# A perceiver block on one core: x and the context also loaded by columns, and the start, the end of the attention and the feed-forward part rearranged

## What is computed

```
x = x + xattn(layernorm(x), ctx)       # ctx has 128 keys, causal mask: query q sees keys <= q, so keys 64..127 never count
x = x + attn(layernorm(x))             # keys and values rebuilt through a 32-wide latent; scores clipped, times a decay, softmax
x = x + ffn(layernorm(x))              # 128 -> 512 -> GELU -> 128
# in ffn both linears quantise input and weight per tensor: q = round(x / scale), scale = max|x| / 127, over the whole tensor
```

## Time and profile before

| | us |
|---|---|
| median of 3 runs | 324.59 |
| lowest, highest | 322.42, 324.89 |
| the profiled execution's own time | 324.61 |
| its span (first to last instruction) | 322.8 |

### The profile page before, as it was taken

The page is one execution under the profiler, slowest core; times in us unless marked ns, Lnnn a source line. Parts: engine busy times, 40 slices in busy tenths (PEclk is TensorE's granted clock), DMA queues, the critical chain, the costliest instruction groups (busy, mean ns, idle before and its releaser), DMA issues.

```text
span 322.8 us, 13785 instructions
## 1 busy us (share of the span) xinstructions
PE 292.3 (91%) x5792; PEld 205.0 (64%) x5792; DVE 256.5 (79%) x561; ACT 250.1 (77%) x544; POOL 226.9 (70%) x176
## 2 busy tenths in 40 slices
PE   4796989999999999999999999999999998575884
PEld 3455757676767676867677777776667767321363
DVE  1486587899977887888788887878788998679883
ACT  3485795868687988787889898889877877499583
POOL 5177576874969697879999999999989970055000
PEclk9798999999999999999999999999999999759999
DMA  8999000000000000000000000000000000000027
GB/s 194 229 199 198 3 2 2 2 4 3 4 2 4 2 4 4 2 4 2 2 4 4 4 4 2 4 3 4 4 2 4 4 3 5 2 0 0 0 66 196
DMA packets 19102, 9.54 MB, mean 30 GB/s; under 512 B 5153, under 2 KB 18786, under 8 KB 19042
## 3 DMA queue, kind: packets, MB, share of 16 engines
q1 hardware_dynamic: 18322, 8.25, 12.0%
q10 hardware_dynamic: 720, 0.43, 0.6%
HBM read 6.57 MB, written 2.10 MB: 27 GB/s over the span
## 4 chain that ended last, share of the span: by engine, by line
PE 75%; ACT 14%; DVE 4%; issue 3%; DMA 1%; ACTq 1%; SPq 0%; DVEq 0%
PE ps L554 13%; PE ps L535 11%; PE ps L581 9%; PE ps L587 8%; PE ps L597 8%; PE ps L475 5%; ACT arena L860 4%; PE ps L459 4%; PE ps L468 4%; PE ps L552 4%; PE ps L566 3%; PE ps L645 2%; PE ps L441 2%; ACT arena L775 2%; DMA arena<-in_ctx 1%
## 5 line engine op out<-in xcount | busy, mean ns | idle before, releaser
L782 ACT ACTIVATE pt<-ps 128x512 f32<-128x512 f32 x128 | 75.9, 594 | 21.7 <-PE ps L554 20.7
L386 POOL TENSOR_TENSOR u<-u,mx 128x1024 f32<-128x1024 f32 x32 | 60.8, 1902 | 37.1 <-DVE mx L991 36.9
L378 POOL TENSOR_TENSOR ud<-u,con 128x1024 f32<-128x1024 f32 x31 | 73.5, 2372 | 1.9 <-DVE u L977 1.9
L972 DVE SCALAR_TENSOR_TENSOR u<-ps,rs,arena 128x1024 f32<-128x1024 f32 x32 | 41.0, 1282 | 20.3 <-PE ps L535 20.2
L535 PE MATMUL ps<-arena,qT 32*64 32x256 f32 x1024 | 44.2, 401 | 6.4 <-ACT arena L775 4.3
L977 DVE TENSOR_SCALAR u<-ps 128x1024 f32<-128x1024 f32 x32 | 39.0, 1220 | 12.5 <-PE ps L535 12.1
L581 PE MATMUL ps<-pt,vx 128*32 128x64 f32 x2048 | 41.0, 221 | 1.7 <-DVE oT L918 1.5
L581 PEld LDWEIGHTS ps<-pt,vx 128*32 128x32 f32 x2048 | 32.2, 110 | 14.8 <-issue 10.0
L587 PE MATMUL ps<-pt,con 128*32 128x128 f32 x1024 | 40.0, 275 | 0.0
L991 DVE TENSOR_REDUCE mx<-u 128x16 f32<-128x1024 f32 x32 | 38.7, 1210 | 0.1
L535 PEld LDWEIGHTS ps<-arena,qT 32*64 32x64 f32 x1024 | 14.9, 129 | 32.2 <-issue 22.5
(11 more groups left out here) (153 smaller groups left out, 568.2 us busy)
## 6 DMA issues: line engine op xcount, KB each, us to landing
out<-pt SPq DMA_DIRECT2D x8, 256.0 KB, 2.3
x<-in_x SPq DMA_DIRECT2D x4, 256.0 KB, 3.6
arena<-in_ctx SPq DMA_DIRECT2D x8, 128.0 KB, 4.1
x<-in_x SPq DMA_DIRECT2D x2, 512.0 KB, 7.0
arena<-in_ctx SPq DMA_DIRECT2D x4, 256.0 KB, 6.6
arena<-in_mask_BxS_if SPq DMA_DIRECT2D x2, 256.0 KB, 5.7
arena<-in_mask_BxS_if SPq DMA_DIRECT2D x4, 64.0 KB, 3.9
arena<-in_mask_BxS_if SPq DMA_DIRECT2D x2, 128.0 KB, 3.8
```

What stands on the lines that cost most here:

```text
L378: pool.tensor_tensor(dh, uh, decay.unsqueeze(1).to_broadcast([P, H, HALF]), ALU.mult)\
L386: pool.tensor_tensor(uh, uh, mx[:, n % 4, 0:count].unsqueeze(2).to_broadcast([P, count, HALF]), ALU.subtract)\
L782: act.activation(pt[:, n % 2, 4 * half:4 * half + 4].rearrange("p h n -> p (h n)"), ps[:, bank, :], ACT.Exp).then_inc(s["emptied"], 1)
L972: dve.scalar_tensor_tensor(by_head(u[:, n % UB]), sc, rs[:, 0, n:n + 1], mask[:, n].unsqueeze(1).to_broadcast([P, H, HALF]), ALU.mult, ALU ...
```

## The change

- `kernel()` also passes x laid out by columns, 128 x 4096, and the first 64 keys of the context by columns, 128 x 4096. `ctx_1024` itself is no longer an input. SP's `load(n)` now issues context columns (into the arena), x columns (into xn3T, which layer one does not use otherwise), x. Pieces "x" and "c" of layer one are gone with their copies; q, k and v of layer one read the loaded columns.
- ACT issues wk, the constants without the identity, wq, the identity, wv. PE starts with 8 matmuls on a zeroed tile (WARM), and the first pieces are k, cq, q. `expand(0, 0)` on ACT comes after cq.
- The last tile's numerators use a bank of the scores (`num_den`); its division comes after the moments of tile 62. The last root is split (28 to 30, and 31).
- The last layernorm: group 6 and tiles 28 to 30 on POOL, tile 31 on DVE. The first maximum's transposes use bank OB and no longer wait for the last copy (L764).
- Up projection: no "minus 1536" pass; instead 32 `open_up` matmuls of 512 columns (weights times -1536) start each accumulation, 8 of them before the first step. The first and last GELU are in two halves. The GELU table is loaded at turn 69.
- Down projection: POOL sums the four blocks of w2 at turns 30 and 31, so one matmul replaces the four of `offset`, and the bias matmul moves to the opening (`open_down`); groups 4 to 7 are opened between later steps. Hidden rounding: ACT 1, 3, 5, 7; POOL 2, 6; DVE 0, 4.

```diff
-LEAD = (("v", 3), ("x", 8), ("c", 7), ("k", 6), ("q", 5))
+LEAD = (("v", 3), ("x", 8), ("k", 6), ("q", 5))
-         ((0, 8), (8, 8), (16, 8), (24, 4), (28, 4)))
-ROOT_TURN = (..., (46, 54, 62, 66, 69))
-APPLY3 = (50, 52, 58, 60, 63, 65, 66, 70)
+         ((0, 8), (8, 8), (16, 8), (24, 4), (28, 3), (31, 1)))
+ROOT_TURN = (..., (46, 54, 62, 66, 67, 69))
+APPLY3 = (50, 52, 58, 60, 63, 65, 67, 70)
-X_ACT = (1, 2, 3)
-H_ACT = (1, 2, 4, 5, 7)
-DVE_TAIL = (("a", 0), ("a", 3), ("f", 0), ("f", 1), ("a", 6)) + tuple(("f", g) for g in range(2, 8))
+WARM = 8
+X_ACT, X_DVE, X_POOL = (1,), (0, 2, 3), (4, 5, 6, 7)
+H_ACT, H_POOL = (1, 3, 5, 7), (2, 6)
+DVE_TAIL = (("a", 0), ("a", 4)) + tuple(("f", g) for g in range(8))
+GELUS = ((0, 0, 1), (0, 1, 2)) + tuple((k, 0, 2) for k in range(1, 15)) + ((15, 0, 1), (15, 1, 2))
...
-    pieces[-1] = [("x", 0), ("cq", 0), ("c", 0), ("q", 0), ("k", 0)]
-    early = ([("v", 0), ("x", 1), ("c", 1)], [("k", 1), ("q", 1)], [("v", 1), ("x", 2)], [("c", 2)], [("k", 2)],
-             [("q", 2)])
+    pieces[-1] = [("k", 0), ("cq", 0), ("q", 0)]
+    early = ([("v", 0)], [("k", 1), ("q", 1)], [("v", 1)], [], [("k", 2)], [("q", 2)])
...
+                sp.dma_start(cT[:, P * t0:P * t1], ctx_cols[0, :, P * t0:P * t1]).then_inc(C_IN[n], 16)
+                sp.dma_start(xn3T[:, P * t0:P * t1], x_cols[:, P * t0:P * t1]).then_inc(XT_IN[n], 16)
                 sp.dma_start(x[:, t0:t1], x_t[:, t0:t1]).then_inc(X_IN[n], 16)
-                for b in range(2):
-                    sp.dma_start(cx[HALF * b:HALF * (b + 1), t0:t1], ctx_t[b, 0:HALF, t0:t1]).then_inc(C_IN[n], 16)
...
+            def last_norm(g, tiles):
+                pool.wait_ge(RS[2], batch_of(2, tiles[-1]))
+                pool.wait_ge(s["filled"], gets_empty(("x3", g - 2)))
+                pool.wait_ge(s["amax_done"], g - 1)
+                for t in tiles:
+                    last = pool.tensor_scalar(xn3[:, g % 2, t % GT], x[:, t], mv[:, 2, t, 0:1], rs[:, 2, t:t + 1],
+                                              ALU.subtract, ALU.mult)
...
+            pool.wait_ge(s["ascale"], 2)
+            pool.wait_ge(s["xr_done"], len(X_DVE))
+            for g in X_POOL:
+                pool.tensor_scalar(x16[g], xn3T[:, g * GT * P:(g + 1) * GT * P], scal[:, 11:12], ROUND16, ALU.mult, ALU.add)
+            pool.wait_ge(s["hscale"], 2)
+            for g in H_POOL:
+                if g >= 6:
+                    pool.wait_ge(s["down_done"], g - 5)
+                pool.tensor_scalar(h16[g % 6], hidden[:, :, g * GT * P:(g + 1) * GT * P], scal[:, 19:20], ROUND16,
+                                   ALU.mult, ALU.add).then_inc(s["hr_done_pool"], 1)
...
+            def open_up(k):
+                for m in range(2):
+                    pe.matmul(ps[:, 2 * (k % 4) + m, :], w1qT[:, k % FC],
+                              minus_off[:, :].unsqueeze(1).to_broadcast([P, GT, P]), start=True, stop=False)
+            def open_down(g):
+                pe.matmul(ps[:, g, :], minus_off[:, :], w2s[:, :].unsqueeze(1).to_broadcast([P, GT, D]), start=True, stop=False)
+                pe.matmul(ps[:, g, :], ones_b[:, :], b2q[:, :].unsqueeze(1).to_broadcast([96, GT, D]), start=False, stop=False)
+            pe.wait_ge(s["warm_set"], 1)
+            for n in range(WARM):
+                pe.matmul(ps[:, OB, :], warm[:, 0:P], warm[:, :], start=True, stop=True)
...
+                if n == NS + LAG_ADD[1]:
+                    open_up(0)
+                    open_up(1)
...
-            pe.wait_ge(s["emptied"], max(fill.values()) + 1)
             pe.wait_ge(s["ared_local"], 1)
-            pe.transpose(ps[0:1, 0, 0:P], scal[:, 8:9], ident).then_inc(s["ared_row"], 1)
+            pe.transpose(ps[0:1, OB, 0:P], scal[:, 8:9], ident).then_inc(s["ared_row"], 1)
...
+            pe.wait_ge(s["emptied"], max(fill.values()) + 1)
+            open_up(2)
+            pe.wait_ge(s["ascale"], 1)
+            open_up(3)
```

More of the change, by code:

```diff
@@ L441, in piece @@
                         last = pe.transpose(ps[:, bank, i * P:(i + 1) * P], src[:, i], ident)
-                if kind == "c":
-                    pe.wait_ge(C_IN[CHUNK[g]], 32)
-                    bank = bank_of(what)
-                    for i in range(GT):
-                        last = pe.transpose(ps[:, bank, i * P:(i + 1) * P], cx[:, g * GT + i], ident)
                 if kind == "cq":
@@ L467, in piece @@
                     bank = bank_of(what)
-                    last = pe.matmul(ps[:, bank, :], wk[:, layer], (xT if layer else cT)[:, j % 2],
+                    last = pe.matmul(ps[:, bank, :], wk[:, layer], xT[:, j % 2] if layer else cT[:, j * GT * P:(j + 1) * GT * P],
                                      start=True, stop=True)
@@ L635, in _ @@
                 if k >= 4:
-                    pe.wait_ge(s["gelu_done"], k - 3)
+                    pe.wait_ge(s["gelu_done"], gelu_count(k - 4))
+                    open_up(k)
                 for m in range(2):
-                    n0 = (2 * pair + m) * GT * P
-                    last = pe.matmul(ps[:, 2 * (k % 4) + m, :], w1qT[:, c], xq[:, n0:n0 + GT * P],
-                                     start=True, stop=True)
-                last.then_inc(s["up_done"], 1)
-            def offset(g):
-                for c in range(FC):
-                    pe.matmul(ps[:, g, :], minus_off[:, :], w2qT[:, c].unsqueeze(1).to_broadcast([P, GT, D]),
-                              start=(c == 0), stop=False)
+                    g = 2 * pair + m
@@ new lines, in _ @@
+                    if c == 0 and g in X_DVE:
+                        pe.wait_ge(s["xr_done"], X_DVE.index(g) + 1)
+                    elif c == 0 and g in X_ACT:
+                        pe.wait_ge(s["xr_done_act"], X_ACT.index(g) + 1)
+                    elif c == 0:
+                        pe.wait_ge(s["xr_done_pool"], X_POOL.index(g) + 1)
+                    pe.matmul(ps[:, 2 * (k % 4) + m, :], w1qT[:, c], x16[g], start=False, stop=True)\
+                        .then_inc(s["up_done"], 1)
@@ L662, in _ @@
                 else:
-                    pe.wait_ge(s["hr_done_dve"], (1 if g == 0 else 1 + sum(e not in H_ACT for e in range(g + 1))))
+                    pe.wait_ge(s["hr_done_dve"], 1 if g == 0 else 3)
                 for i in range(GT):
@@ L833, in _ @@
                 weights(n)
+                if n == ROOT_TURN[2][-1]:
+                    act.activation(scal[:, 31:32], cst[:, 0:1], ACT.Gelu, bias=cst[:, 0:1])
                 if n == 24:
@@ L849, in _ @@
                             expand(j, h)
-            act.activation(scal[:, 31:32], cst[:, 0:1], ACT.Gelu, bias=cst[:, 0:1])
             act.wait_ge(s["ascale"], 2)
@@ L993, in _ @@
                 for tile in due(n, LAG_PV):
-                    if tile != EARLY:
+                    if tile not in (EARLY, NS - 1):
                         divide(tile)
```

246 lines of the change are left out of this document (142 added, 104 removed).

## The result

| | before | after |
|---|---|---|
| median (lowest to highest) | 324.74 us (322.42 to 325.02), 4 runs | 316.16 us (314.52 to 318.24), 4 runs |
| profiled execution: own time, span | 324.61, 322.8 | 315.6, 313.7 |
| forecast | | 309.5, range 305 to 315 |

What follows compares the result with a forecast made beforehand. PE's work in the attention was taken as the bound, with chains of little overlap at the start and before the first GELU. 324.6 - 3.9 (layer one) - 7.0 (start) - 4.2 (tail) = 309.5 us; range 305 to 315.

Steps and rivals of the forecast that it cites:

- Part 2: The start: loaded columns replace transposes and copies, so first reading and turn 4 come earlier; 7.0 us gained, bounds 3.4 and 9.
- Rival B: At the start, the extra bytes delay each chunk up to load 3; 313.1 us in all, chance 0.11.
- 0.7 for the clock: Around turn 4: PE still waits some 2.5 us before it, so half of the low clock's 1.5 us is gained.
- Part 1: Steady layer one, groups 4 to 7 without x and c pieces: 0.97 us saved a group, 3.9 in all.
- It fits, barely: Layer one, turns 10 to 16: DVE's 2.0 us of idle time suffices against about 1.5 that PE saves.
- Rival C: DVE becomes the bound of layer one, whose gain is then 1.9 us; 311.5 us in all, chance 0.08.
- Part 3: From the last values to the first GELU: POOL's norms become the limit, GELU starts 2.0 us earlier, bounds 0 and 3.
- Part 4: First GELU to the second maximum's transpose: 0.3 us from the halved GELU, 0.9 from fewer matmuls ahead of the transpose.
- Part 5: The down projection: engines would gain 2 us, the stores leave 1.0; bounds -2 and 2.
- 8 x 0.9: Down projection: PE does each of eight groups in 0.9 us, within 8.3 us from the first rounded half.
- ready well before PE is at groups 2 and 6: Down projection: POOL's two roundings, 2.8 us each, are done before PE needs them.
- rival A: Down projection: POOL and DVE shut each other out, DVE's second half waits for POOL's 2.8 us; 312.3 us, chance 0.21.

Runs made afterwards that it cites:

- experiment 4: The changed kernel with eight matmuls of zeros at the end of turn 3, where PE waits for ACT: 314.81 us, ratio 0.9729.
- experiment 1: The changed kernel with POOL's two roundings waiting for DVE's three: 312.47 us, ratio 0.964; with the groups also shared anew: 314.38 us, ratio 0.9713.
- inverse first: The changed kernel with ACT taking the inverse of the denominator ahead of the first exponent in layer one: 314.62 us, ratio 0.9728.
- the best one: The changed kernel with turn 3's fill, inverse first, last norms on DVE, POOL's rounding behind DVE's, new sharing, PE kept busy, eight output slots: 309.18 us.

## Why the prediction was right and where it was wrong

**Direction and cause** were right: the start and the groups of layer one carry the gain, and the time around the span is the same (1.8 and 1.9).

**Part 2** came out in its sum: 6.6 of 7.0. Read of the scores, the mask as its last wait and turn 4 were each met within 0.3 us; the first scores came at 9.19, not near 8.5, hidden behind the mask. Rival B fell: the queue moved 306 GB/s. But the sum holds an error that another one covers. The way to turn 4 gave 5.8 (5.5 forecast), and turns 4 to 7 gave 0.83 (20.48 to 19.65), where 1.0 for group 3's transposes and 0.7 for the clock had been counted. So of the 0.7 for the clock nothing came: the stretch at 0.50 was about as long as before (3.4 us, 3.2 before), and experiment 4 shows that 1.6 lay there. Half of the matmuls' low-clock time was the wrong model, as before turn 4 it all went or all stayed in each profiled run.

**Part 1** failed in its sentence "It fits, barely". The sum of DVE's idle time over seven turns was compared with the sum of PE's savings. But the savings come in single turns, behind a fixed order of DVE work of 1.28 + 0.28 + 1.21 + 0.28 us; idle time elsewhere in the window can't be used there. Rival C had the engine, and nearly the size (2.5 measured, 1.9 priced), at a chance of 0.08; its "only turns 10 to 16" was too narrow, as turns 9 and 21 lost time too. Also the pieces were priced too high: PE's busy time fell by 0.83 a group on average, not 0.97.

**Part 3** was right about POOL (the norms are its 5.5 us, and they hold the maximum), and its number is an error of adding: its own terms, 0.65 for the transpose and 0.9 to 1.4 less 0.3 behind it, give 1.25 to 1.75, not the 2.0 taken. Measured are 1.5, of which 0.84 come up to the transpose and 0.65 behind it, where the openings between the scale and the first data matmul took 1.89 us in part at low clock. **Part 4**: the 0.9 behind DVE's last maximum came (0.26 us are left of 1.19). The 0.3 in front didn't: DVE starts 0.4 sooner behind the first GELU's start, but its eighteen maxima end 18.8 us after their start instead of 18.1.

**Part 5** is the main failure, 3.1 us, by two steps. The step "8 x 0.9" took the full clock for granted. Taking away the `offset` matmuls ahead of the second maximum (counted as a gain in part 4) left PE idle for 3.1 us, and the down projection began at half the clock: 1.2. The second is "ready well before PE is at groups 2 and 6", which let POOL's roundings run beside DVE's at no cost. That is rival A, which had 0.21: POOL's 2.50 us (2.8 forecast) shut out DVE's rounding. By the Trainium skill, page "SBUF — State Buffer", section "Who interferes with whom", POOL and DVE, in a form of DVE that uses both of its port pairs, hold the pair that they share exclusively for a whole instruction. The trace agrees, with 2.39 us against 0.75 for the same rounding, and for POOL's first piece 2.50 us where its second, with no DVE rounding beside it, took 1.97. With the change's sharing of the groups it cost 2.1 on the path; the wait's own part of that is shown only up to the first store, 1.4 to 1.6. The rest of part 5 held: it forecast 14.2 us from the rounding to the end (15.2 less 1.0), and with both steps mended and the groups shared anew it is 14.0.

With the parts as measured the forecast becomes 309.5 + 0.4 + 1.4 + 0.5 + 0.55 + 3.1 = 315.5, and the profiled execution took 315.6; the median of the four runs is 316.16. In the prediction's terms that is A, C and a low clock in the down projection, which no rival held, together. The rivals were priced one at a time, while the range had to hold two or three of them together.

## What to carry to other kernels

Where a bound engine gets relief, take the queue of the second engine for each single turn, and look where its last step stands against what the first waits for; a sum of idle time over many turns says only that it may fit. Before an engine's filler work is taken away, look whether it kept the clock up for the work behind it. And give no POOL instruction of several us the same start as a DVE rounding from SBUF on the path: one changed wait (experiment 1) brought the first store 1.4 us nearer to the start of the rounding.

## What the runs showed of the hardware that was not expected

Before turn 4 PE stood still for 2.3 to 2.8 us, and a low clock followed in eleven of the twelve profiled runs that had no filling matmuls there (turn 4 of 5.1 to 5.8 us, the kernel before among them), in one it didn't. That run (inverse first) waited 2.48 us, no less than the others, and took 3.80 for turn 4. Its windows, and the changed kernel's below, with the granted clock before the DMA share:

```profile
22.00:24.00 2.00, 0.95 (x40) 0.56 (x44) 0.75 (x5) 1.00 (x2) 1.92 (x2) 1.00 1.07 153
24.00:26.00 2.00, 2.00 (x51) 1.80 (x40) 2.00 (x3) 0.93 (x3) 2.00 (x2) 1.00 0.95 218
```

```profile
22.00:24.00 2.00, 1.17 (x28) 0.48 (x32) 0.63 (x5) 0.78 (x2) 1.92 (x2) 0.77 0.91 150
24.00:26.00 2.00, 2.00 (x50) 1.58 (x43) 1.26 (x1) 0.24 (x1) 2.00 (x2) 0.50 1.00 201
```

A clock of 0.50 is the lower of the two levels, 1.2 GHz. That kernel's profiled span is 1.4 us shorter than the changed kernel's, and 1.3 of it stand at turn 5; its median is 1.5 lower, but whether its other runs kept the clock too no trace shows. Why it kept the clock is open. With the fill in place all five profiled runs had 3.8, and the runs of one kernel lay closer together: 0.6 us for the best one, 3.7 for the changed kernel.
